# Four drive terms of a recurrence made by ScalarE and TensorE, in a convolution-attention kernel

## The reference

```python
xp, z = x @ W_in                       # 64 -> 2 x 128 channels, over 1024 tokens
xc = silu(xprev * conv_w[:, 0] + xp * conv_w[:, 1] + conv_b)
dt_r, Bc, Cc = split(xc @ W_x)         # 8, 16, 16
dt = softplus(dt_r @ W_dt + b_dt)
A = -exp(A_log)                        # 128 x 16
def step(h, inp):                      # h: 128 channels x 16 states
    dA = exp(dt_t[:, :, None] * A)
    h = dA * h + (dt_t * x_t)[:, :, None] * B_t[:, None, :]
    y = einsum('bds,bs->bd', h, C_t)
y = (y + D * xc) * silu(z)
out = y @ W_out
```

## Time and profile before

| | |
|---|---|
| time, median of 3 runs | 944.47 us (943.37 to 945.66) |
| the profiled execution's own time | 945.53 us |
| its span, first to last instruction | 943.8 us |
| recurrence, from the first scan to the last | 27.2 to 481.5 us of the span |
| granted PE clock, mean | 0.957 |

### The profile page before, as it was taken

One profiled execution on the slowest core, in us unless ns is written; L12 is line 12 of the kernel. 1 busy time (PEld: TensorE's weight loads), 2 busy tenths in 40 slices (PEclk: granted clock), 3 DMA queues, 4 the chain that ended last, 5 costly groups with the idle time before them and its releaser, 6 DMA issues. The chain is left out here.

```text
span 943.8 us, 10168 instructions
## 1 busy us (share of the span) xinstructions
PE 829.2 (88%) x2974; PEld 487.8 (52%) x2974; DVE 711.9 (75%) x767; ACT 508.9 (54%) x702; POOL 549.7 (58%) x373
## 2 busy tenths in 40 slices
PE   5579897979899898985587899989999999999997
PEld 1224342433333333332134554548888888888886
DVE  1999999999999999999965445655666655566655
ACT  4645666556566566643315456555555554555554
POOL 4678989999998998976736965303222121222120
PEclk9799999999999999997987999999999999999999
DMA  7959897889969898896609800001433433233433
GB/s 177 335 211 331 312 334 276 339 285 330 324 255 367 312 321 307 288 325 230 209 0 134 162 0 1 1 1 46 134 106 117 134 94 130 90 105 118 134 96 82
DMA packets 75924, 178.22 MB, mean 189 GB/s; under 512 B 24578, under 2 KB 25620, under 8 KB 75876
## 3 DMA queue, kind: packets, MB, share of 16 engines
q1 hardware_dynamic: 75892, 177.85, 57.8%
HBM read 175.57 MB, written 2.26 MB: 188 GB/s over the span
## 5 line engine op out<-in xcount | busy, mean ns | idle before, releaser
L455 POOL TENSOR_TENSOR prod<-hidden,c_wide 128x1024 f32<-128x1024 f32 x128 | 300.2, 2358 | 64.1 <-DVE hidden L888 60.4
L551 PE MATMUL ps_y<-prod,ident 128*128 128x512 f32 x512 | 242.7, 618 | 31.7 <-POOL prod L455 31.5
L888 DVE TENSOR_TENSOR_SCAN hidden<-decay,ps_d 128x1024 f32<-128x1024 f32 x92 | 209.9, 2282 | 8.3
L1923 PE MATMUL ps_conv<-hankel,u_high 128*128 128x512 f32 (+1 forms) x768 | 215.3, 361 | 0.0
L551 PEld LDWEIGHTS ps_y<-prod,ident 128*128 128x128 f32 x512 | 98.1, 197 | 172.0 <-issue 116.7
L1923 PEld LDWEIGHTS ps_conv<-hankel,u_high 128*128 128x128 f32 x768 | 138.6, 189 | 25.5 <-DVE u_t L1786 0.2
L1923 PE MATMUL ps_conv<-hankel,u_low 128*128 128x512 f32 (+1 forms) x384 | 138.1, 360 | 0.0
L2040 DVE TENSOR_TENSOR stack<-ps_conv,stack 64x512 fp32r<-64x512 f32 x128 | 88.3, 690 | 62.0 <-ACT stack L2007 59.6
L1751 POOL CAST block_mix<-even 128x256 fp32r (+1 forms) x32 | 12.7, 398 | 208.5 <-PE sums L1792 208.5
L2040 DVE TENSOR_TENSOR qk<-ps_conv,qk 64x512 fp32r<-64x512 f32 x128 | 88.3, 690 | 50.2 <-ACT qk L2007 47.5
L874 DVE TENSOR_TENSOR ps_d<-ps_x,b_wide 128x1024 f32<-128x1024 f32 x92 | 113.4, 1232 | 4.6
(11 more groups left out here) (283 smaller groups left out, 1154.5 us busy)
## 6 DMA issues: line engine op xcount, KB each, us to landing
b_wide<-bc_rows SPq DMA_DIRECT2D x128, 512.0 KB, 5.6
c_wide<-bc_rows SPq DMA_DIRECT2D x128, 512.0 KB, 5.3
hankel<-filters SPq DMA_DIRECT2D x32, 1026.0 KB, 5.2
plus<-in_M_phi_plus SPq DMA_DIRECT2D x2, 1024.0 KB, 12.8
minus<-in_M_phi_minus SPq DMA_DIRECT2D x2, 1024.0 KB, 18.0
x_pair<-in_x SPq DMA_DIRECT2D x2, 768.0 KB, 8.2
...
```

Of the source, the lines that this page charges most:

```text
L455: nc.gpsimd.tensor_tensor(prod[k % PAIR][:, :], hidden[k % DEEP][:, :], c_wide[s % BC_DEEP][:, :], ALU.mult).then_inc(prod_ready, 1)
L551: mm = nc.tensor.matmul(out, ident[:, :], halves(prod[k % PAIR])[h], start=False, stop=(k % N == N - 1))
L888: nc.vector.tensor_tensor_scan(hidden[k % DEEP][:, order], left[:, order], right[:, order], 0.0, ALU.mult, ALU.add).then_inc(hidden_ready, 1)
L1923: mm = nc.tensor.matmul(out, pairs[q][wp][:, 2 * delta + source, :], rows, start=(delta == 0 and term == 0), stop=(delta == 2 * half + 1 a ...
```

## The change

State by state, the drives are spread over one more way:

- states 2, 4, 8, 11 are *turned* (in the last unit 2 and 7): tokens are put on partitions. PE transposes `dtx` (two halves of four 128x128 tiles, `turn_late` and `turn_early`) and the B rows into `ps_w`; ACT takes them to SBUF as `dtx_t` and `b_t` (`take_turned`). With tokens on partitions B is one value for each partition, so ACT makes a drive by eight 128x128 copies with a scale pointer (`scale_drive`), and PE transposes it back into `ps_d` (`turn_drive`), where the scan reads it.
- states 3, 7, 10, 15 are shared with POOL (before: 2, 3, 6, 9, 15; in the last unit 6 in both).
- z is projected behind conv (`gate_in` waits for `xc`), so its silu reads `ps_w` and no copy of z is made. `xc` has one buffer instead of two.
- D * xc is written to `ps_y` by ACT (`skip_in`), where PE added it with a diagonal matrix.
- relu stays in `ps_w`, and PE no longer adds it. `add_exponential` and `add_logarithm` stand one state later.
- decays 11, 12, 13 stand ahead of the softplus passes on ACT; decay 6 stands behind the two silus.
- `b_wide` has three buffers and 12 loads a unit. `norm_scale` moves from state 3 to state 1 on DVE.

The core of the diff:

```diff
-POOL_STATES = (2, 3, 6, 9, 15)
-WIDE_SHARED = POOL_STATES[1:4]
-DRIVE_OF = {2: 0, 3: 1, 6: 0, 9: 1, 15: 0}
+POOL_STATES = (3, 7, 10, 15)
+TURNED_STATES = (2, 4, 8, 11)
+WIDE_SHARED = POOL_STATES[0:3]
+DRIVE_OF = {3: 0, 6: 1, 7: 1, 10: 0, 15: 1}
+B_DEEP = 3
...
                 def gate_in(u, i, b):
-                    pe.wait_ge(dtx_ready, u)
+                    pe.wait_ge(xc_ready, u + 1)
                     project(i, b, w_gate[i], z_ready)
...
+                def turn_late(u):
+                    pe.wait_ge(dtx_kept, u + 1)
+                    turn_dtx_half(1)
+                    for t in range(TILES):
+                        mm = nc.tensor.transpose(ps_w[:, t * C:(t + 1) * C], dt_low[BC_ROW:, t * 128:(t + 1) * 128],
+                                                 ident[BC_ROW:, BC_ROW:])
+                    mm.then_inc(dtx_turned, 1)
+                def turn_early(u):
+                    pe.wait_ge(dtx_t_ready, 3 * u + 2)
+                    turn_dtx_half(0)
+                def turn_drive(u, s, last=False):
+                    scanned(u, s - (2 if s - 1 in wide(last) else 1))
+                    for half in range(2):
+                        pe.wait_ge(drive_t_ready, 2 * turned_before(u, s, last) + half + 1)
+                        for t in range(half * SPANS, (half + 1) * SPANS):
+                            mm = nc.tensor.transpose(ps_d[:, t * 128:(t + 1) * 128], drive_t[turned_slot(s, last)][:, t, :], ident[:, :])
+                    mm.then_inc(drive_turned, 1)
...
                             if s == Y_LAG:
+                                turn_drive(u, s - 1, not ahead)
                                 if i == 0 and not first:
                                     out_product(b - 1)
+                                if s + 1 in turned(not ahead):
+                                    turn_drive(u, s + 1, not ahead)
+                                if i == 0 and not first:
                                     conv_in(v, j, bv)
...
+                            if s > Y_LAG and s + 1 in turned(not ahead):
+                                turn_drive(u, s + 1, not ahead)
+                            if s == 0:
+                                turn_early(u)
...
+                def skip_in(u, i, taken=0):
+                    at_least(act, gated_ready, u)
+                    at_least(act, g.mixed_ready, taken)
+                    nc.scalar.activation(ps_y[:, :], xc[:, :], ACT.Copy, scale=cols[i][:, 1:2]).then_inc(skip_ready, 1)
...
+                def scale_drive(u, s, last=False):
+                    act.wait_ge(dtx_t_ready, 3 * u + 3)
+                    at_least(act, drive_turned, turned_before(u, s, last) - 1)
+                    for t in range(TILES):
+                        part = nc.scalar.activation(drive_t[turned_slot(s, last)][:, t, :], dtx_t[:, t, :], ACT.Copy, scale=b_t[:, t, s:s + 1])
+                        if t % SPANS == SPANS - 1:
+                            part.then_inc(drive_t_ready, 1)
...
+                            if s == 0:
+                                shared_decay_of(u, i, WIDE_SHARED[0], dtx_t_ready, 3 * u + 3)
+                                scale_drive(u, 2)
+                                decay_of(u, i, 2)
+                            if s == 1:
+                                scale_drive(u, 4)
+                                decay_of(u, i, 4)
                             if s == 2:
+                                decay_of(u, i, 5)
...
+                                silu_input(v, j)
                                 silu_gate(v, j)
                                 nc.scalar.preload_act_table_set("natural_log_exp_and_others")
                             if s == 4:
-                                shared_decay_of(u, i, WIDE_SHARED[1], xc_ready, v + 1)
+                                decay_of(u, i, 6)
+                                shared_decay_of(u, i, WIDE_SHARED[1], gate_ready, v + 1)
...
                             if s == N - 1:
-                                shared_decay_of(u, i, POOL_STATES[4], hidden_ready, u * N + POOL_STATES[4])
+                                shared_decay_of(u, i, POOL_STATES[3], hidden_ready, u * N + POOL_STATES[3])
                                 keep_dtx(v)
                                 decay_of(v, j, 1, last and i == 0)
+                                take_turned(v)
...
-                            if s in shared(final) and s in WIDE_SHARED:
-                                drive_step(u, s + 1, final)
-                            elif s not in shared(final) and not (s - 1 in shared(final) and s - 1 in WIDE_SHARED):
-                                drive_step(u, s, final)
+                            if s not in shared(final) + turned(final):
+                                drive_step(b, i, s, last)
```

More of the change, by code:

```diff
@@ L249, in mamba_stage @@
         soft = sb("soft", [D, L])
-        rectified = sb("rectified", [D, L])
+        dtx_t = sb("dtx_t", [128, TILES, D])
+        drive_t = [sb(f"drive_t_{i}", [128, TILES, D]) for i in range(2)]
+        b_t = sb("b_t", [128, TILES, N])
         minus_ident = sb("minus_ident", [128, 128])
-        skip = [sb(f"skip_{d}", [D, D]) for d in DIRS]
         one_plus = a.late[:, 0:L]
@@ L307, in shared_before, with turned_before, spread_order, b_slot @@
             return SHARE * u + sum(p < s for p in shared(last))
+        def turned_before(u, s, last=False):
+            return TURNED * u + sum(p < s for p in turned(last))
+        def spread_order(last):
+            return [(i, s) for i in range(2) for s in range(N) if s not in turned(last and i == 1)]
+        UNIT_LOADS = N - TURNED
+        def b_slot(i, s, last):
+            return spread_order(last).index((i, s)) % B_DEEP
+        def b_loads(b, i, s, last):
+            return 16 * (2 * UNIT_LOADS // B_DEEP * b + spread_order(last).index((i, s)) // B_DEEP + 1)
+        def turned_slot(s, last):
+            return turned(last).index(s) % 2
         def own_states(last):
@@ L705, in softplus_exp @@
                     if not first:
-                        nc.scalar.activation(rectified[:, :], ps_w[:, :], ACT.Relu).then_inc(relu_ready, 1)
+                        nc.scalar.activation(ps_w[:, :], ps_w[:, :], ACT.Relu).then_inc(relu_ready, 1)
                     act.wait_ge(abs_ready, u + 1)
@@ L735, in decay_of, with shared_decay_of @@
                                          scale=a_neg[i][:, s:s + 1]).then_inc(decay_ready, 1)
-                def shared_decay_of(u, i, s, taken, count):
+                def shared_decay_of(u, i, s, taken, count, final=False):
                     act.wait_ge(taken, count)
-                    nc.scalar.activation((ps_w if s in WIDE_SHARED else ps_d)[:, :], dt[i][:, :], ACT.Exp,
+                    nc.scalar.activation((ps_w if s in wide(final) else ps_d)[:, :], dt[i][:, :], ACT.Exp,
                                          scale=a_neg[i][:, s:s + 1]).then_inc(share_decay, 1)
@@ L829, in _ @@
                 keep_dtx(0)
[L830 to L832 removed]
+                take_turned(0)
                 batch(0, first=True)
```

217 lines of the change are left out of this document (122 added, 95 removed).

## The result

The changed kernel takes 961.56 us (median of 4 runs, 961.17 to 968.97); the kernel before, beside it, 945.07. The ratio is 1.0189 with a 95% interval of 1.0139 to 1.0239: it is slower, by 1.4 to 2.4%, where 940.5 was forecast.

A forecast was written before the change was run, and what follows sets the result against it. DVE's recurrence bounds the kernel, with ACT's list holding scan 6 back after the change. Unit terms of -7.7 us and +3.6 for PE's clock gave -4.1, from 945.53 to 941.4, then about 940.5 against the median; range 928 to 953.

The forecast's parts named there:

- What hides the rest: Section on hidden waits: B loads mostly released at least 7 us ahead of their reader, so three buffers cost nothing.
- the loads of B come late: Rival, chance 0.06: with three buffers B loads are late; at 1 us a unit the kernel takes 948 us.
- At `i` = 0, without the residual, it is on time: End of unit: scan 15, 1.3 us late at `i` = 1, does not wait at `i` = 0.
- Scan 6 waits for decay 6: DVE stalls for ACT: 2.1 us at `i` = 0, 3.0 at `i` = 1, plus 1.2 there for PE's low clock.
- The scale pass: ACT's eight 128x128 copies making a turned drive: 2.36 us (1.93 to 3.1), four a unit 9.4.
- Units with `i` = 0: Units 2, 4 and 6: 50.2 us of DVE's work plus 2.2 us waiting at scan 6, 52.4 each.
- Units 3 and 5: Units with `i` = 1: 55.2 us each before the low clock's 1.2, 1.3 of it for a late scan 15.
- The start: Unit 0: scan 2's turning makes it slower, but DVE's expert weights cover ACT there; about -2.3 us.
- The last unit: Unit 7: two drives go from DVE, -2.5 us.
- The clock: PE idles between drives 2 and 4 at `i` = 1 and slows: 1.2 us in each of three units, +3.6.
- The rival that put this at the change of unit: Chance 0.22: PE idles about 2 us before `turn_late` and slows, 2.7 us a unit, giving 954 us.
- The drain at a table switch: Rival, chance 0.02: each ACT table load also drains for as long as the load, 15 us more, 957 us.

The follow-up runs named there:

- e2_four: The changed kernel with a fourth wide-B buffer, the store order on SP kept: 967.68 us, ratio 1.0253 to the kernel before.
- e7_store_four: e1_store with a fourth wide-B buffer: 950.11 us, ratio 1.0041 to the kernel before.
- e8_control: e1_store, but with the group norm's store left ahead of the load of B 10: 966.3 us, ratio 1.0215 to the kernel before.
- e1_store: The changed kernel with the group norm's store moved from s == 9 to s == 12 on SP, its followers later: 950.16 us, ratio 1.0058 to the kernel before.
- e3_decay6: The changed kernel with decay 6 on ACT right behind decay 5, ahead of the silus: 964.67 us, ratio 1.0204 to the kernel before.
- e4_both: The moved store of e1_store and the early decay 6 of e3_decay6 together, on the changed kernel: 950.19 us, ratio 1.0045 to the kernel before.
- e0_after: The changed kernel as it is, run again beside the experiments: 969.39 us, ratio 1.0262 to the kernel before.
- e5_pe: e1_store with PE turning dtx's first half ahead of sum 13 and, in the second direction, conv and z ahead of sums 0 and 1: 950.05 us, ratio 1.0047.

## Why the prediction was wrong

**The step that failed** is in "What hides the rest": "each load is released at least 7 us ahead of its reader", and from it "three buffers cost nothing". It looked at when a buffer comes free and not at what stands ahead of the load on SP. The buffer for B 10 was free in time: with the store moved, its load left at D+25.05, 9.4 us ahead of POOL's share. But by the prediction's own list of ACT (decay 6 done at D+26.0, then a decay, a scale pass, a decay and the squares: 1.08 + 2.36 + 1.08 + 1.23) the squares end at D+31.8, where they had ended at 26.9; measured 32.75. SP, which works in order, has an instruction that waits for them just ahead of that load. The prediction looked at SP for waits on buffers, and not for this wait on ACT. The conclusion on the buffers was right (e2_four, e7_store_four); the loads were late all the same. Taking it away was worth 19 us beside the same kernel before (969.39 to 950.16), 14 from e8_control's 20.5 above the kernel before to e1_store's 6.7 above it, and 10 from the 16.5 of the changed kernel's first runs. The rival "the loads of B come late", at 1 us a unit and put down to three buffers, named neither this cause nor its price.

"At `i` = 0, without the residual, it is on time", said of scan 15, did not hold either. With the store in the way `dt_x` waits 0.45 us at the end of unit 4 and 3.17 at the end of unit 6. With the store moved `dt_x` does not wait there, but scan 15 does, 1.09 us behind unit 4 of e1_store as behind unit 3, for the reason given for the units with `i` = 0 below.

**The rest of the sum** can be read from e1_store, whose span (946.3) is 6.6 above the forecast's 939.7:
- *Scan 6 waits for decay 6*: forecast 2.1 and 3.0 + 1.2, measured 2.40 and 3.74 (units 4 and 5 of e1_store), right within 0.5. That it cannot simply be moved away, e3_decay6 and e4_both show: decay 7 is next on ACT, and drive 8 on PE.
- *The scale pass*: forecast 2.36, measured 2.43 to 2.45. Decay 11 at `i` = 1: 0.7 forecast, 0.75 measured (unit 5 of e1_store). `turn_early` behind the sum: 1.9 of ACT forecast, 2.04 measured.
- *Units with `i` = 0*: 52.4 forecast, 53.4 to 53.7 without the store's wait, 1.0 to 1.3 too little each. The term is scan 15 of the unit before, the first scan behind D. The list of ACT had its decay done at D+1.24, but ACT makes decay 0 ahead of it and is done at D+2.23 (unit 4 of e1_store, 251.36); in the kernel before the scan followed `dt_x` without a wait:

```profile
251.45 2.29 DVE L998 TENSOR_TENSOR_SCAN hidden<-ps_d,drive 128x1024 f32<-128x1024 f32 x1 [1.09 <-ACT ps_d L823]
```

- *Units 3 and 5*, where 1.3 us was charged for that scan: 56.4 forecast, 56.29 and 55.64.
- *The start*: a gain of 2.3 forecast, D(1) at 84.28 measured, 2.5 too little. The expert weights, behind scan 3, hide ACT there, but scan 2 waits 3.96 for its turned drive and scan 6 3.54, and PE comes cold to both: the first eight transpositions take 2.19 and the sum of state 0 3.75 us.
- *The last unit*: -2.5 forecast, -0.1 measured after. Its two drives fell away, but scan 15 waits 1.01 and the attention's first steps 1.89 for POOL in place of 0.61.

**The clock.** After 2.99 us of idling PE ran eight transpositions in 1.97 in e1_store, where 1.09 is usual, and 2.42 for a sum in place of 1.88: 0.9 + 0.5 = 1.4 where 1.2 was charged. The rival that put this at the change of unit did not come: PE idled 0.81 to 0.89 us there and not about 2, and in each of the units 1 to 6 of the changed kernel four transpositions there took 0.65 or 0.66 and the sum 1.98 or 1.99, the full level. The section "HAM oscillation — how this bites in real kernels" of "TensorE: Matmul & The Clock Gate" in the Trainium skill, that a pause between groups makes the next group slow, agrees with the turn of drive 4 at `i` = 1; at the change of unit, where the pause was under 1 us, nothing was slowed in the changed kernel. In unit 5 of e5_pe, where PE pauses a second time there, the granted clock did fall, to 0.66 from 306 to 309 us; in its units 3 and 4 the same order ran at the full level.

**The drain at a table switch** did not come either: the load at 280.87 takes 1.28 us and decay 6 starts at 282.16, 0.01 later; the silu ahead of the load ended at 280.85. The figure of the Trainium skill for the draining ("ScalarE: Activation LUTs", section "What ACT_TABLE_LOAD costs") is not borne out here.

**How far the clock explains the rest.** With the store in the way a unit with `i` = 0 is as long as PE is slow behind its wait for product 8. Where the sum of state 8 takes 1.98 us, the unit takes 55.7 to 56.3 (unit 2 of e0_after, units 2, 4 and 6 of e3_decay6). In the other such units of the changed kernel, e0_after, e2_four and e8_control the sum takes 3.1 to 3.8: where `dt_in` behind it takes at most 2.3, the unit takes 57.8 to 58.7, and where `dt_in` takes 3.8 too, 61.1 to 62.7. With the store's wait gone it takes 53.4 to 53.7 (e1_store). So the late share costs 2 to 3 us in a unit by itself, and up to 6.4 more through PE's clock. Between executions of the changed kernel the time goes with the mean granted clock of the run: 961.2 to 964.1 us at 0.949 to 0.952, and 968.8 to 971.3 at 0.942 to 0.946. That makes the clock the likely reason for the 8 us between its medians, but no execution of 961 us has a profile, so it is not shown.

**What stays open**: why the clock falls there in one execution and not in another. The idle time ahead of the sum does not tell them apart. PE in unit 2 of e0_after:

```profile
184.31 1.98 PE L607 MATMUL ps_y<-prod,ident 128*128 128x512 f32 x4 [2.62 <-POOL prod L494]
```

PE in unit 2 of the changed kernel's first profile:

```profile
183.08 3.58 PE L607 MATMUL ps_y<-prod,ident 128*128 128x512 f32 x4 [2.65 <-POOL prod L494]
```

The runs were made on more than one chip, and no run tells whether the chip has a part in it.
